# Attention b of a hybrid block on one Trainium2 core: blocks of 8 queries, and the score products on 64x64 tiles of the array

## The reference, cut to what matters

```python
q, k, v = (heads(Wq), heads(Wk), heads(Wv))
att_rel_pos = jnp.einsum('bhsd,pd->bhsp', q, pos_emb_k)
att_idxs = jnp.clip(i[None, :] - i[:, None], -R, R - 1) % P      # R = 128, P = 256
att_pos = jnp.take_along_axis(att_rel_pos, att_idxs[None, None, :, :], axis=3)
attn_val = jnp.einsum('bhsd,bhtd->bhst', q, k) + att_pos
att = jax.nn.softmax((attn_val + att_pos) * attn_scale, axis=-1)
y = jnp.einsum('bhst,bhtd->bhsd', att, v)
```

## Time and profile before

| | |
|---|---|
| median of 3 runs | 6808.61 us (6804.55 to 6820.63) |
| profiled execution, its own time | 6812.0 us |
| its span in the profile | 6810.2 us |
| TensorE busy (matmuls) | 5638.8 us, 83% |
| VectorE busy | 4866.3 us, 71% |
| ScalarE busy | 3638.3 us, 53% |
| GpSimd busy | 1430.9 us, 21% |
| mean granted clock of TensorE | 0.823 |

### The profile page before, as it was taken

One profiled execution on the slowest core, in us unless ns is written; L12 is line 12 of the kernel. 1 busy time (PEld: TensorE's weight loads), 2 busy tenths in 40 slices (PEclk: granted clock), 3 DMA queues, 4 the chain that ended last, 5 costly groups with the idle time before them and its releaser, 6 DMA issues. The chain is left out here.

```text
span 6810.2 us, 110274 instructions
## 1 busy us (share of the span) xinstructions
PE 5638.8 (83%) x28670; PEld 3857.3 (57%) x28670; DVE 4866.3 (71%) x16015; ACT 3638.3 (53%) x11201; POOL 1430.9 (21%) x1970
## 2 busy tenths in 40 slices
PE   4787887778777777877799997888888888889998
PEld 3344444444434444444588885555555555578887
DVE  4788888878878787888688885555555555478887
ACT  3677777777767777778322223444444444422222
POOL 1011011101101110110244442111111111144444
PEclk6657666666667666666899999999999999999999
DMA  1000000000000000000234431000000000034434
GB/s 50 1 1 1 1 1 1 1 1 1 1 1 1 1 1 1 1 1 1 51 79 85 88 81 25 5 5 5 5 5 5 5 5 5 3 76 88 85 78 100
DMA packets 236353, 161.24 MB, mean 24 GB/s; under 512 B 84835, under 2 KB 232838, under 8 KB 235910
## 3 DMA queue, kind: packets, MB, share of 16 engines
q1 hardware_dynamic: 235910, 157.33, 11.3%
HBM read 146.52 MB, written 10.49 MB: 23 GB/s over the span
## 5 line engine op out<-in xcount | busy, mean ns | idle before, releaser
L732 ACT ACTIVATE junk<-SS,nt 128x256 bf16<-128x256 f32 x3072 | 1514.0, 497 | 23.8 <-DVE SS L852 17.5
L1191 ACT ACTIVATE f_th<-bank 128x256 f32<-128x256 f32 x1088 | 418.0, 384 | 1146.8 <-PE bank L1122 1146.8
L593 PE MATMUL bank<-ident,prob 128*128 128x128 f32 x2048 | 463.1, 366 | 636.6 <-DVE prob L914 635.6
L1091 POOL TENSOR_TENSOR f_hid<-f_g_m,f_cbs 128x256 f32<-128x256 f32 x1024 | 744.5, 727 | 850.5 <-DVE f_g_m L1336 649.5
L593 PEld LDWEIGHTS bank<-ident,prob 128*128 128x128 f32 x2048 | 296.3, 182 | 942.4 <-DVE prob L914 849.9
L571 PE MATMUL bank<-k,q 8*128 8x256 f32 x2048 | 817.7, 575 | 12.0 <-DVE SS L852 12.0
L1635 ACT COPY pTb<-bank 128x512 f32<-128x512 f32 x512 | 300.2, 586 | 961.8 <-PE bank L1488 961.8
L1488 PE MATMUL bank<-ident,prob 128*128 128x128 f32 x2048 | 582.6, 285 | 278.4 <-ACT prob L1657 277.0
L604 PE MATMUL bank<-pT,vaug 128*32 128x256 f32 x2048 | 785.8, 526 | 20.7 <-ACT pT L742 20.7
L1121 PE MATMUL bank<-f_xTf,wgT 128*128 128x256 f32 x2176 | 692.1, 400 | 52.2 <-DVE f_g_m L1336 36.6
L1734 DVE TENSOR_REDUCE mxb<-bank 128x2 f32<-128x512 f32 x512 | 352.5, 688 | 532.0 <-PE bank L1502 518.3
(11 more groups left out here) (229 smaller groups left out, 9574.0 us busy)
## 6 DMA issues: line engine op xcount, KB each, us to landing
f_cbs<-f_shares SPq DMA_DIRECT2D x512, 256.0 KB, 5.8
qrow<-q_rows SPq DMA_DIRECT2D x1024, 4.0 KB
q_rows<-qTb SPq DMA_DIRECT2D x32, 128.0 KB, 1.7
out_dram<-xres SPq DMA_DIRECT2D x4, 1024.0 KB, 9.3
f_shares<-f_combT SPq DMA_DIRECT2D x64, 32.0 KB, 1.5
px<-pext SPq DMA_DIRECT2D x16, 15.5 KB
nat<-in_L_attn_a_W_qkv_dram SPq DMA_DIRECT2D x3, 64.0 KB
bqk<-in_L_attn_a_b_qkv_dram SPq DMA_DIRECT2D x8, 0.1 KB
```

What stands on the lines that cost most here:

```text
L593: last = nc.tensor.transpose(PT[h % 2][:, k * T + i * P:k * T + (i + 1) * P], prob[:, h % 2, i, k * P:(k + 1) * P], ident[:, :])
L732: nc.scalar.activation(junk[:, c % 2, :], SS[:, uu % 4, c, :], ACT.Sign, bias=bias(c), accum_out=acc[:, k, uu % 4, c:c + 1]).then_inc(s["s ...
L1091: pool.tensor_tensor(hid[:, e % NBUF, :], g_m[:, e % NBUF, :], cbs[:, par, e, :], ALU.mult).then_inc(s["hid"], 1)
```

## The change: what it does

- A block has J = 8 queries, so there are A = 32 blocks. `q1` and `q2` have 8 heads times 8 queries = 64 columns per block and half the elements.
- Rows 0 to 63 of the array hold heads 0 to 7, rows 64 to 127 heads 8 to 15. `mask_h8` serves both. `qrow` has 16 groups of 8 partitions, place j of the lower heads and then of the upper ones; `px` has the table once for each of these. The loads of `qrow` become 16.
- A pair p of units (one for each half of the heads) covers four blocks. Its products are 16 matmuls on 64x64 tiles, at all four positions of the array: row half by half of the heads, column half by block. The lower heads write bank `S[2p % 4]`, the upper ones `S[(2p+1) % 4]`.
- There are four score banks and four buffers `probb`; one bank M takes the place of M0 and M1, one bank O that of two.
- TensorE transposes two units in a row, then makes the products of the pair p+2, then weighs (at four of eight pairs, four steps at a time), then does the small jobs. Transposes and products are no longer interleaved; a semaphore increment stands between them.
- The scale is put into `qTb`, the maximum is negated by the reduction itself, and `nb` goes.
- On ScalarE the exponentials of a unit stand ahead of the copy of the unit two before.

```diff
-J = 16
+J = 8
...
+        HH = H // 4
+        PAIRS = A // 4
+        PER = PAIRS // HALVES
+        UNITS = 2 * PAIRS
+        KEYS = 2 * J
...
-        S = bank[0:2]
-        PT = bank[2:4]
-        O = bank[4:6]
-        M0, M1 = bank[6], bank[7]
+        S = bank[0:4]
+        PT = bank[4:6]
+        O, M = bank[6], bank[7]
...
+        SLOT = {"xT'": 0, "qk'": 1, "n1": 2, "v'": 3, "oT": 4, "y": 5, "n0": 7}
+        WEIGH = {0: (1, 0), 1: (1, 4), 4: (0, 0), 5: (0, 4)}
...
-                    for hg, landed in enumerate(("qa", "qb")):
-                        if b >= 1:
-                            sp.wait_ge(s["qz"], 2 * (b - 1) + hg + 1)
-                        heads = slice(HG * hg, HG * (hg + 1))
-                        for j in range(J):
-                            sp.dma_start(qrow[HD * j:HD * (j + 1), heads, :],
-                                         scr[par, heads, :, j, :].rearrange("h d a -> d h a")).then_inc(s[landed], 16)
+                    if b >= 1:
+                        sp.wait_ge(s["qz"], 2 * b)
+                    for n in range(KEYS):
+                        heads = slice(HG * (n // J), HG * (n // J + 1))
+                        sp.dma_start(qrow[HD * n:HD * (n + 1), :, :],
+                                     scr[par, heads, :, n % J, :].rearrange("h d a -> d h a")).then_inc(s["qd"], 16)
...
-                def products(b, u, par):
+                def products(p, par):
+                    pe.sem_inc(s["turned"], 1)
                     for i in range(2):
-                        a = 8 * ((u // 4) % 2) + 2 * (u % 4) + i
-                        o = S[u % 2][:, i * T:(i + 1) * T]
-                        nc.tensor.matmul(o, q1[:, a, heads, :], kTb[:, par, :], start=True, stop=False)
-                        yield
-                        last = nc.tensor.matmul(o, q2[:, a, heads, :],
-                                                px[:, (A - 1 - a) * J:(A - 1 - a) * J + T], start=False, stop=True)
+                        for kind in range(2):
+                            for hg in range(2):
+                                rows = slice(64 * hg, 64 * (hg + 1))
+                                for c in range(2):
+                                    a = 4 * p + 2 * i + c
+                                    off = (A - 1 - a) * J
+                                    last = nc.tensor.matmul(S[(2 * p + hg) % 4][64 * c:64 * (c + 1), i * T:(i + 1) * T],
+                                                            (q1, q2)[kind][rows, a, :, :],
+                                                            kTb[rows, par, :] if kind == 0 else px[rows, off:off + T],
+                                                            start=(kind == 0), stop=(kind == 1), tile_position=(64 * hg, 64 * c))
+                                if i == 1 and kind == 1:
+                                    last.then_inc(s["scores"], 1)
@@ TensorE's batch @@
+                    for p in range(PAIRS):
+                        transposes(b, 2 * p)
+                        transposes(b, 2 * p + 1)
+                        if p + 2 < PAIRS:
+                            if p + 2 == PER:
+                                pe.wait_ge(s["q1"], 2 * b + 2)
+                                pe.wait_ge(s["qz"], 2 * b + 2)
+                            products(p + 2, par)
...
+                        if p in WEIGH:
+                            g, k0 = WEIGH[p]
+                            for k in range(k0, k0 + 4):
+                                if g == 0:
+                                    weigh(b, par, g, k)
+                                elif prev:
+                                    weigh(b - 1, 1 - par, g, k)
+                        for w in slots(p, prev, more):
@@ ScalarE's batch @@
+                    for p in range(PAIRS):
+                        if p == 3 and prev:
+                            take_sums(b - 1, 1)
+                        for hg in range(2):
+                            exponentials(b, 2 * p + hg)
+                            if p >= 1:
+                                copy_pt(b, 2 * (p - 1) + hg)
+                            elif prev:
+                                copy_pt(b - 1, UNITS - 2 + hg)
+                        for w in slots(p - 1, prev, more):
@@ VectorE's batch @@
+                    for p in range(PAIRS):
+                        for hg in range(2):
+                            u = 2 * p + hg
+                            dve.wait_ge(s["scores"], UNITS * b + u + 1)
+                            V.tensor_reduce(nmx[:, u % 4, :], S[u % 4][:, :].rearrange("p (i t) -> p i t", i=2), AX, ALU.max,
+                                            negate=True).then_inc(s["nmax"], 1)
```

More of the change, by code:

```diff
@@ L1381, in build @@
-        M0, M1 = bank[6], bank[7]
-        LOADS = 16 * J
-        STORES = 16
[L1385 to L1394, removed]
+        probb = bb_("probb", [P, 4, 2, T])
@@ new lines, in build, with use @@
+        SLOT = {"xT'": 0, "qk'": 1, "n1": 2, "v'": 3, "oT": 4, "y": 5, "n0": 7}
+        FIRST = 3
+        OLD = ("n1", "oT", "y")
+        WEIGH = {0: (1, 0), 1: (1, 4), 4: (0, 0), 5: (0, 4)}
+        def use(b, what):
+            order = list(SLOT)
+            if not isinstance(b, int):
+                return len(SLOT) * b + order.index(what)
+            if b == 0:
+                return FIRST + [w for w in order if w not in OLD].index(what)
+            if b == BATCH - 1:
+                order = [w for w in order if w[-1] != "'"]
+            return len(SLOT) * b + order.index(what)
@@ L1396, in batches, with slots @@
+        def slots(p, prev, more):
+            return [w for w, at in SLOT.items() if at == p and (prev or w not in OLD) and (more or w[-1] != "'")]
         def batches(eng, batch, end):
@@ L1508, in weigh @@
-                def weigh(b, par, g, j):
-                    if j == 0:
-                        pe.wait_ge(s["pt"], PAIRS * b + 4 * g + 4)
-                        if g % 2 == 0:
-                            wait(pe, s["oc"], 2 * b + (g // 2 - 1))
-                    hg, half, t = g // 2, g % 2, j % 2
+                            o = PT[u % 2][:, t * T:(t + 1) * T].rearrange("p (h i c j) -> p i c h j", h=HG, i=2, c=2)[:, i]
+                            last = nc.tensor.transpose(o, probb[:, u % 4, i, t * P:(t + 1) * P], ident[:, :])
@@ L1610, in _ @@
+                batches(pe, batch, lambda: None)
+                for k in range(2 * HH):
+                    weigh(BATCH - 1, 1, 1, k)
+                turn_sums(BATCH - 1, 1, LAST)
+                turn_o(BATCH - 1, LAST + 1)
+                project_o(LAST + 2)
             @block.scalar
@@ L1638, in take_sums, with exponentials @@
-                def take_sums(b, hg):
-                    act.wait_ge(s["pv"], 4 * b + (2 * hg + 2))
-                    nc.scalar.copy(osumb[:, hg, :, :].rearrange("p c i -> p (c i)"), O[hg][:, :]).then_inc(s["oc"], 1)
+                        i = nc.scalar.copy(oT[:, :], M[:, 0:T])
+                    i.then_inc(s["mc"], 1)
+                def exponentials(b, u):
+                    act.wait_ge(s["nmax"], UNITS * b + u + 1)
+                    wait(act, s["pused"], UNITS * b + u - 3)
+                    for i in range(2):
+                        last = nc.scalar.activation(probb[:, u % 4, i, :], S[u % 4][:, i * T:(i + 1) * T], ACT.Exp,
+                                                    bias=nmx[:, u % 4, i:i + 1], scale=1.0)
+                    last.then_inc(s["exp"], 1)
@@ L1710, in normalise @@
[L1710 to L1716 removed]
+                        dve.wait_ge(s["scores"], UNITS * b + (8 * half - 8))
```

341 lines of the change are left out of this document (143 added, 198 removed).

## The result

The changed kernel takes 6063.48 us (median of 4 runs, 6032.13 to 6070.41) against 6806.58 us (4 runs): ratio 0.890, 95% interval 0.886 to 0.893. The forecast was 6162 us. The direction came out, and so did the array's part of the sum; the size was 99 us short.

A forecast was written before the change was run, and what follows sets the result against it. Attention b was held bound by order inside a unit, TensorE waiting on ScalarE. Array work of 31.6 us, raised by issue to 34.9 and waiting to 35.0 per batch against 55.2, gave 6166, adjusted to 6162 us; range 6060 to 6510.

The forecast's parts named there:

- the array's part of the sum: TensorE in attention b: transposes, products, tiling changes, weighing and small jobs keep the array working or turning 31.6 us per batch.
- Issue: TensorE's sequencer in attention b: 472 passes at 0.065 us plus some 42 marks at 0.1, 34.9 us per batch.
- What bounded the kernel before: Attention b: no engine full; order inside a unit matters, with TensorE waiting in a 3.45 us cycle, 16 times a batch.
- the ring: Attention b's unit: TensorE block, ScalarE copy, then exponentials before the next block; 3.45 us, with TensorE idle 0.71 us.
- Products, 13.8 us with four tiles: Attention b's score matmuls: four 64x64 tiles run together, 64 rounds of 0.216 us per batch, down from 27.6 us.
- 55.2 us per batch before: Attention b's batch period from a once-per-batch instruction over 31 periods; 32 batches taken as 1766 us.
- The sign named for a right forecast: In attention b's trace, the once-per-batch instruction would have a period of 33 to 37 us.
- VectorE, ScalarE, M, DMA, GpSimd, cost nothing: Attention b: other engines' work, the single bank M and the qrow loads stay covered within 35 us per batch.
- the tightest places: Pairs p = 2 and 3, where q/k copies and take_sums precede exponentials on ScalarE: at worst half a microsecond.
- Rival 1: Attention b's products: row halves take turns, only two tiles at a time; 45.9 us per batch, 6510 us; chance 0.11.
- Rival 3: Attention b's products: weight loads stand in front of each stream, 7 us more per batch, 6287 us; chance 0.08.
- Rival 4: TensorE issue takes 0.11 us per pass: 56 us per batch, 6830 us, no change; chance 0.04.

The follow-up runs named there:

- unrolled_weigh_twice: Changed kernel with attention b's loop written out and weighing in two stretches of 64 passes per batch instead of four of 32; median 5985.0 us, ratio 0.880.
- split_columns: Against unrolled_weigh_twice, each product of 256 columns cut into two of 128, giving 728 passes per batch in place of 472; 5972.2 us.
- rows_shared: Against the changed kernel, both halves of the heads use array rows 0 to 63, so only two tiles can work at once; 6467.1 us.
- order_and_no_nb: Kernel before with ScalarE's exponentials ahead of the copy and the nb multiplication removed (reduction negates, scale in qTb); median 6672.3 us, ratio 0.981.

## Why the direction was right and the size 99 us short

The step that failed is the term *Issue*: the prediction took 34.9 us per batch for the sequencer's pace, above the 31.6 in which the array has to work, and the runs showed that the array alone bounds a batch, at 31.0 us. The second error is the stage before, taken as 1766 us and measured as 1828. In the prediction's own terms:

- *What bounded the kernel before*: right. Reordering ScalarE alone gave 4.7 us per batch, and took 3.7 of TensorE's 8.6 idle us. In the other 4.9 TensorE waits mostly for exponentials, and these for VectorE, which GpSimd holds up; the prediction counted that hold-up only as work that goes with `nb`. With the four banks, which it mentioned only as the thing that ends the ring, 0.1 us of idle time is left (unrolled_weigh_twice).
- *Products, 13.8 us with four tiles*: right. A round takes 0.216 us, and taking half the rows away costs 13.2 us.
- *Transposes, products, changes of tiling, weighing, small jobs, 31.6 us in sum*: 31.0 measured.
- *Issue, 34.9 us*: this is the term that failed. 0.065 us per pass was an upper bound from two marks between which TensorE's queue was probably full; I took the bound as the value. The bound was not worked out evenly either: with 0.1 us for each of the two marks, as in the sum of 42 marks, it is (1.4 - 0.2) / 20 = 0.060, and the term 32.5 us. split_columns has 0.042 sustained without a loss, so at most 19.8 us for 472 passes. The Trainium skill (TensorE: Matmul & The Clock Gate, "Wait — 56ns, not 53.3ns?") gives some 62 ns per MATMUL with hardware decode off. This case's 42 ns are below that, so that limit did not apply here; which setting the chip had, no run shows. Its closeness to my 65 was a coincidence that made the wrong value look sound.
- *55.2 us per batch before*: mis-sized. The instruction of the earlier trace rows belongs to the next batch's preparation, and its first period is 23.8 us; the other 30 have a mean of 56.2. The stage took 1828 us, not 32 x 55.2 = 1766.
- *The loop*: not in the prediction. It costs 48 us.

The account: the forecast had a gain of 646 us. The stage before was 62 us longer than taken; the stage after was 1058 us, not 32 x 35.0 = 1120, another 62. Of the 35.0 us per batch 4.0 were too much (issue 3.3, the array's sum 0.6, waits 0.1), 128 us in all, and the loop's 48 and some 18 of first and last batch too little. That makes 770; attention a happened to take 28 us more in the profiled execution, which leaves the 741.5 of the spans. So part of the nearness is luck: the loop that nobody had foreseen hid 48 us of the error, and attention a 28 more. The sign named for a right forecast, a period of 33 to 37 us, did not come; the fours of passes with 0.22 us between them did.

- *VectorE, ScalarE, M, DMA, GpSimd, cost nothing*: right for the 31.0 us period. The one wait seen is that of p = 3 for ScalarE's copy, 0.3 us per batch, which the prediction had among the tightest places. GpSimd's multiplications take 2.1 us, not 1.9.
- *Rival 1* (two tiles at a time) was priced at 45.9 us; the kernel that enforces it has 44.2. *Rival 3*, and the sentence of the Trainium skill behind it (same page, Part 3, "The mechanism"), are refuted for 64x64 tiles as well: in rows_shared all tiles have the same rows, and with loads ahead of each stream a round could not take 0.216 us.
- *Rival 4* (0.11 us per pass) is refuted by the same 0.042.

## What to carry to other kernels

Tiling the array pays only if the consumers' latency is off its path: here 64x64 tiles with two score banks gave 1.7 us per batch, four banks and the new order at the old array time of the products gave 12 (rows_shared), and all together 25. Removing an instruction that is held up by another engine need not remove the hold-up: without `nb`, the mask multiplication met it. Before an upper bound from one row becomes the value of a term, test it or keep the array's own sum as the likeliest. After a loop body has grown in instructions or shrunk in time, look at the branch back and at the DMA transfers of kind "instruction": they tell whether the body is fetched in every round. A stage whose own code is unchanged can be hit too.

## What the runs showed of the hardware beyond what was expected

- TensorE's branch back takes 0.21 us in loops of up to 1477 records and 3.6 us in loops of 1998 and 2949. In attention b's loop the body of 1998 goes with 126 fetches of 16 KB, the body of 1477 with none of these.
- Behind 6 of 14 stops of 1.9 to 2.4 us TensorE's passes ran at the lower clock (transposes 0.21 us apart, not 0.11), behind the other 8 they did not.
- Two programs that differ from the kernel before only in how attention b's batches are looped lose 146 us in a later stage. VectorE stops there 14 times for 10.3 to 11.1 us, each time behind its own branch back, with 70 fetches of instructions where the kernel before has 2.
- A VectorE multiplication of 3.64 us took 5.04 to 6.40 where order_and_no_nb had it beside a GpSimd one of 3.88 us; a maximum read from PSUM at such a time still took 0.69 (at 4995.07 us of that run).
- TensorE took 728 passes in 30.7 us, 0.042 us per pass, 0.1 us more than for 472.
